# Moving the pieces of projections and feed-forward among the 64 slots of a batch

## Chip, cores and metric

The kernel runs on one core of a Trainium2 chip. The metric is the device time of one execution in microseconds (us), the median of the runs shown. All of the work is one program; eight batches are computed one after the other.

## What is computed

For each of 8 batches with 1024 tokens of 256 features:

```python
xn = layernorm(x)
# attention branch, 16 heads of 16 features
u, v, q, k = split(silu(xn @ W1 + b1), 4)              # each 1024 x 256
scores = q_h @ k_h.T                                    # per head, 1024 x 1024
attn   = silu(scores) / S
y_attn = layernorm((attn @ v_h) * u, gamma, beta) @ W2 + b2
# feed-forward branch, hidden width 1024, ternary weights
h = gelu(layernorm(xn, g1, b1) @ ternary(w1).T + fb1)
y_ffn = layernorm(h, g2, b2) @ ternary(w2).T + fb2
out = x + y_attn + y_ffn
```

Everything is float32. Products that need the accuracy are split into a high and a low part in fp32r and summed over several matmul passes.

## The kernel before, in words

The attention of one batch is cut into `GROUPS` = 64 groups, called slots here. A slot g (function `scores`, L890 to L905) multiplies 128 keys with 512 queries for four pairs of heads: four matmuls, two at a time, into the four PSUM banks `scores`. ScalarE turns these into `attn` with two Silu activations of 128x1024 each (`silu_group`, L538). TensorE multiplies them with `V` one slot later (`times_v`, L907 to L923: four matmuls of 32 columns, written as eight instructions for two output positions in the profile's merged rows). There is one set of score banks: the first half of the next scores waits for the first Silu of this slot, the second half for the second.

Between `scores(g)` and `times_v(g-1)` TensorE issues the steps that row g of `TABLE` names. The same table is walked by ScalarE, VectorE and GpSimd, each doing its own part of a step in the table's order (`body` of each engine; SyncE has a fixed order of its own, L429 to L443). So the table is a schedule written out by hand, and every engine is strictly in order. The steps are:

- `xn.i`, `xt.i` (i = 0 to 3): normalise 256 tokens of the next batch, transpose them, split them into `xp` (L710, L948, L564, L820).
- `k.c.h`, `q.c.h`, `u.c.h`, `v.i`: projections (L958, L967); ScalarE applies Silu to k, q, u (L544), VectorE splits k and q into parts (L826, L828) and moves v to `vraw` (L836). `vs.c` places v in `V` on ScalarE (L556).
- `y.i`, `f1.t.h`, `gelu.i`, `ln2.i`, `nrm2.i`, `g.t.r`, `f2.t`: the feed-forward branch. `y` (L766 to L773, VectorE) is its input, `f1` the first product in two halves for each of 8 token tiles, evacuated at L779, `gelu` two tiles at once on ScalarE (L582, with a table load before and after it), `ln2` the statistics (L696, L700, and GpSimd L480, L482), `nrm2` the normalisation (L791), `g` four transposes (L985) with three VectorE operations (L796, L801, L803), `f2` the second product with 16 matmuls (L992), added to `part` (L807).
- `zt.i`, `zs.i`, `a.i`: the end of the previous batch's attention branch: transpose for the statistics (L1002, L732, L736), split (L741, L743), the product with W2 (L1008), added to `part` (L750).
- `px` (L757): `part` is set to x plus a constant for the present batch. It waits until the output of the previous batch has been stored (L756, `s_out`).

TensorE's pieces (`zt a u f1 g f2 xt k q v`) use two PSUM banks `fill` in turn. A piece waits for the evacuation of the piece two before it.

k and q do not go straight to the matmuls. SyncE writes the parts `kst` and `qst` to scratch in HBM (`write_parts`, L396 and L399, two DMAs each) and, after both have landed, reads them back in the layout of the score matmuls (`load_stack`, L416 and L419, ten DMAs) for one half c of the heads and one half h of the tokens. `scores` of slot 0 waits for stack (0,0), slot 4 for stack (0,1), slots 32 and 36 for (1,0) and (1,1). Stacks (0,0) and (0,1) of a batch are made from `k.0.0 q.0.0` and `k.0.1 q.0.1` in the last slots of the batch before. All these DMAs go through SyncE's one queue, in order: the stacks, `load_x`, and the two stores of the previous batch's output (L427), which wait for `a.1` and `a.3`.

Batches 1 to 6 are a hardware loop (`Fori`, L878 for VectorE and the same on the other engines), batch 0 and batch 7 are written out before and behind it. A prologue (`PRO`) runs the steps for the first batch (`ln1 xn xt k.0 q.0 v vs.0`) in the order in which they stand in the table, an epilogue (`EPI`) the steps `zs zt a` of the last.

The change and the steps of the prediction touch `TABLE` (L58 to L123), and through it the order of everything above. Which piece uses which `fill` bank follows from its place in the table (`bank_of`, L171).

Of the kernel before, what the change touches and what calls it, by code (L numbers as in the profile page):

```python
# [56 lines left out]

TABLE = (  # L58
    "zs.0 zt.0 zs.1 zt.1",
    "a.0 zs.2",  # L60
    "a.1",
    "zt.2",
    "zs.3 zt.3",
    "a.2",
    "vs.1 a.3 u.1.0 k.1.0 y.0",
    "q.1.0",
    "u.1.1",
    "k.1.1",
    "u.0.1 px q.1.1 u.0.0 y.2",
    "f1.0.0",  # L70
    "f1.0.1",
    "y.1",
    "",
    "f1.1.0 f1.1.1 y.3 gelu.0",
    "f1.2.0 f1.2.1",
    "ln2.0",
    "nrm2.0",
    "f1.3.0 g.0.0",
    "g.0.1",
    "f1.3.1 f2.0",  # L80
    "g.1.0",
    "g.1.1 gelu.1 f1.4.0 f1.4.1",
    "ln2.1 f2.1 f1.5.0",
    "nrm2.1 f1.5.1",
    "g.2.0",
    "g.2.1",
    "f2.2",
    "g.3.0",
    "",
    "",  # L90
    "g.3.1 f1.6.0 gelu.2",
    "f2.3 f1.6.1 f1.7.0",
    "ln2.2 f1.7.1",
    "",
    "",
    "nrm2.2 ln1",
    "",
    "g.4.0",
    "g.4.1 xn.0",
    "f2.4 g.5.0 g.5.1 gelu.3 xt.0",  # L100
    "f2.5 xn.1",
    "xt.1",
    "ln2.3",
    "nrm2.3",
    "k.0.0",
    "g.6.0 xn.2",
    "g.6.1",
    "q.0.0",
    "f2.6",
    "g.7.0",  # L110
    "g.7.1",
    "xt.2",
    "xn.3 v.0",
    "v.1 xt.3",
    "",
    "",
    "",
    "f2.7",
    "k.0.1",
    "q.0.1",  # L120
    "v.2",
    "v.3 vs.0",
)  # L123
SLOTS = [[(n.split(".")[0], *map(int, n.split(".")[1:])) for n in row.split()] for row in TABLE]
assert len(SLOTS) == GROUPS
# [981 lines left out]
```

## Time and profile before

| what | value |
|---|---|
| median of 3 runs | 1669.28 us (1665.27 to 1671.85) |
| the profiled execution | 1665.21 us, its span 1663.4 us |
| TensorE busy | 1542.5 us, 93% of the span |
| ScalarE busy | 1226.5 us, 74% |
| VectorE busy | 896.1 us, 54% |
| GpSimd busy | 98.6 us, 6% |
| mean granted TensorE clock | 0.982 of 2.4 GHz |
| Silu of the scores, L538 | 1024 activations, 985.3 us |
| `times_v` L921 and `scores` L902 | 550.9 and 414.9 us busy (overlapping pairs and fours) |

How to read it: an engine that is busy 93% of the span is not at its peak, because matmuls are pipelined and their ends are modelled. A slot is therefore measured here from the start of its first score matmul to that of the next slot's; the rows of the timeline give these starts. In the timeline, "idle before" in square brackets is the time for which the engine waited, and behind the arrow stands what ended it; "issue" is a wait for nothing that the profile shows. PE is TensorE, PEld its weight loads, DVE VectorE, ACT ScalarE, POOL GpSimd, SPq the DMA issues of SyncE.

### The profile page before, as it was taken

Reading aid. Unit: us, or ns where it says so; the run is one execution under the profiler, and the core shown is the slowest. Engines: PE = TensorE matmul, PEld = TensorE weight load, DVE = VectorE, ACT = ScalarE, POOL = GpSimd, SP = SyncE. Lnnn points to the kernel's source line nnn. Section 1 sums busy time; section 2 is a strip of 40 time slices with the busy share of each in tenths; the row PEclk is TensorE's granted clock in tenths of the full one; section 3 lists DMA queues with packets and bytes.
Section 4 is the critical chain, followed back from the end, with each engine's and each line's share of the span. In section 5 each row is a group of like instructions: output and inputs, shape, how many; then the busy total and the mean of one; then the engine's idle time right before and its main releaser. Section 6 shows DMA issues by size and latency. Waiting matters only on the chain.

```text
span 1663.4 us, 27784 instructions
## 1 busy us (share of the span) xinstructions
PE 1542.5 (93%) x9826; PEld 760.8 (46%) x9826; DVE 896.1 (54%) x1716; ACT 1226.5 (74%) x1285; POOL 98.6 (6%) x193
## 2 busy tenths in 40 slices
PE   4799999999899998999989999799997999999997
PEld 3345445444454444444444444444444454544443
DVE  5365735666257553576435664366634657346553
ACT  2378877788668886778857797587875788767884
POOL 2000100000000100001000010000100001000000
PEclk9799999999999999999999999999999999999999
DMA  6470044601544034430335203361034700346000
GB/s 192 90 151 27 6 88 115 123 26 38 110 99 87 26 68 87 127 77 1 77 90 134 57 1 77 90 152 39 1 79 101 152 26 13 88 103 127 1 1 26
DMA packets 62330, 123.68 MB, mean 74 GB/s; under 512 B 7664, under 2 KB 9328, under 8 KB 61168
## 3 DMA queue, kind: packets, MB, share of 16 engines
q1 hardware_dynamic: 62192, 121.81, 32.2%
q8 instruction: 90, 1.47, 0.4%
q14 instruction: 48, 0.39, 0.1%
HBM read 79.84 MB, written 41.94 MB: 73 GB/s over the span
## 4 chain that ended last, share of the span: by engine, by line
issue 75%; PE 15%; POOLq 4%; ACT 3%; DMA 1%; DVE 1%; POOL 1%; SPq 0%; DVEq 0%; ACTq 0%
PE outs L921 5%; PE scores L902 4%; ACT attn L538 2%; POOLq L505 2%; PE fill L992 2%; PE fill L976 1%; PE fill L958 1%; PE fill L985 1%; POOLq L497 1%; POOL rs L491 1%; POOLq L481 1%; DMA QS<-q_scratch 1%; PE fill L1008 0%; DMA q_scratch<-qst 0%; PE fill L967 0%
## 5 line engine op out<-in xcount | busy, mean ns | idle before, releaser
L538 ACT ACTIVATE attn<-scores 128x1024 f32<-128x1024 f32 x1024 | 985.3, 1025 | 361.3 <-PE scores L902 360.9
L921 PE MATMUL outs<-attn,V 128*32 128x512 f32 x4096 | 550.9, 610 | 0.3 <-ACT attn L538 0.3
L902 PE MATMUL scores<-QS,KS 64*128 64x512 f32 x2048 | 414.9, 467 | 57.4 <-ACT attn L538 28.6
L902 PEld LDWEIGHTS scores<-QS,KS 64*128 64x128 f32 x2048 | 172.6, 186 | 533.8 <-ACT attn L538 391.7
L796 DVE TENSOR_TENSOR tmp<-fill,l2g 128x512 f32<-128x512 f32 x128 | 88.5, 691 | 129.6 <-PE fill L985 125.9
L921 PEld LDWEIGHTS outs<-attn,V 128*32 128x32 f32 x4096 | 81.2, 109 | 129.8 <-issue 118.3
L992 PE MATMUL fill<-Wq,hgh 128*128 128x256 f32 x512 | 131.5, 295 | 0.6 <-DVE tmp L796 0.5
L958 PE MATMUL fill<-xp,W1h 128*128 128x512 f32 x384 | 127.9, 415 | 3.0 <-DVE xp L820 3.0
L779 DVE SCALAR_TENSOR_TENSOR hid<-fill,ratq,fb1b 128x512 f32<-128x512 f32 x128 | 96.1, 751 | 61.5 <-PE fill L976 50.8
L992 PE MATMUL fill<-Wq,hgl 128*128 128x256 f32 x512 | 125.2, 282 | 0.0
L992 PEld LDWEIGHTS fill<-Wq,hgh 128*128 128x128 f32 x512 | 97.2, 190 | 18.9 <-issue 16.7
L807 DVE SCALAR_TENSOR_TENSOR part<-fill,cq,part 128x256 f32<-128x256 f32 x64 | 31.0, 484 | 136.2 <-PE fill L992 135.1
L480 POOL TENSOR_TENSOR rp<-mv,epst 128x2 f32<-128x2 f32 x64 | 12.5, 195 | 1500.5 <-DVE mv L700 961.8
L992 PEld LDWEIGHTS fill<-Wq,hgl 128*128 128x128 f32 x512 | 97.4, 190 | 0.3
L803 DVE TENSOR_TENSOR hgl<-tmp,hgh 128x512 fp32r<-128x512 f32 x128 | 88.6, 692 | 9.9 <-issue 0.4
L985 PE MATMUL fill<-ident,hid 128*128 128x128 f32 x512 | 83.4, 285 | 2.9 <-DVE hid L791 1.8
L696 DVE BATCH_NORM_STATS2 st<-hid 128x6 f32<-128x512 f32 x128 | 79.1, 681 | 10.6 <-issue 5.6
L958 PEld LDWEIGHTS fill<-xp,W1h 128*128 128x128 f32 x384 | 67.4, 190 | 35.2 <-issue 22.5
L958 PE MATMUL fill<-xp,W1l 128*128 128x512 f32 x192 | 75.7, 394 | 0.0
L985 PEld LDWEIGHTS fill<-ident,hid 128*128 128x128 f32 x512 | 54.1, 141 | 40.1 <-issue 37.0
L976 PE MATMUL fill<-Wq,yX 128*128 128x512 f32 x256 | 72.2, 413 | 0.0
L976 PE MATMUL fill<-Wq,yT 128*128 128x512 f32 x256 | 71.2, 410 | 0.0
(110 smaller groups left out, 1383.2 us busy)
## 6 DMA issues: line engine op xcount, KB each, us to landing
QS<-q_scratch SPq DMA_DIRECT2D x128, 256.0 KB, 7.2
k_scratch<-kst SPq DMA_DIRECT2D x64, 256.0 KB
q_scratch<-qst SPq DMA_DIRECT2D x64, 256.0 KB
KS<-k_scratch SPq DMA_DIRECT2D x64, 256.0 KB, 4.9
KS<-k_scratch SPq DMA_DIRECT2D x128, 128.0 KB, 5.7
xin<-in_x SPq DMA_DIRECT2D x8, 1024.0 KB, 4.8
out_dram<-part SPq DMA_DIRECT2D x16, 512.0 KB, 2.7
w1raw<-in_W SPq DMA_DIRECT2D x1, 1024.0 KB, 7.1
```

What stands on the lines that cost most here:

```text
L505: pool.drain()
L538: nc.scalar.activation(attn[:, g % 2, 2 * hf:2 * hf + 2, :], SP[:, 2 * hf:2 * hf + 2, :], ACT.Silu).then_inc(s_silu, 1)
L696: V_.bn_stats(st[:, j, n, :] if len(views) > 1 else st[:, j, :], v)
L779: V_.scalar_tensor_tensor(out=hid_of(t)[:, cols], in0=FP[:, k, :], scalar=ratq[:, t:t + 1], in1=fb1b[:, cols], op0=ALU.mult, op1=ALU.add). ...
L796: V_.tensor_tensor(tmp[:, :].rearrange("p (c n) -> p c n", n=P), FP[:, k, :].rearrange("p (c n) -> p c n", n=P), l2g[:, 4 * r:4 * r + 4].u ...
L803: V_.tensor_tensor(hgl[:, r, :], tmp[:, :], hgh[:, r, :].bitcast(F32), ALU.subtract).then_inc(s_hg, 1)
L902: ins = mm(SP[:, j, :], KS[rows, pair, t * P:(t + 1) * P], QS[rows, pair, h * HALF:(h + 1) * HALF], start=True, stop=True)
L921: ins = mm(OP[32 * j:32 * j + 32, g // RUN % 2, :], V[:, t, c * HPC // 2 + j, o * DH:o * DH + 2 * DH], attn[:, g % 2, n, :], start=(o == 0 ...
L958: ins = mm(bank.rearrange("p (i n) -> p i n", i=2), w[:, kc, col:col + P], xp[:, 2 * h:2 * h + 2, part, kc, :], start=n == 0, stop=n == le ...
L976: ins = mm(bank, y_of(t // 2)[:, part, kc, t % 2 * P:(t % 2 + 1) * P], Wq1[:, kc, hf * HALF:(hf + 1) * HALF], start=n == 0, stop=n == len( ...
L985: ins = nc.tensor.transpose(bank[:, n * P:(n + 1) * P], hid_of(t)[:, col:col + P], ident[:, :])
L992: ins = mm(bank[:, 0:D], w[:, r, n * P:(n + 1) * P], Wq2[:, 4 * r + n, :], start=i == 0, stop=i == len(passes) - 1)
```

## The change

Only `TABLE` changes. The same 96 steps of a batch stand in other rows; none is added or dropped. Rows with no entry go from 9 to 10. The `f2` rows stand further apart in the middle of the batch. `k.0.1` and `q.0.1`, which had rows 60 and 61, both go into row 63, behind `v.3`; `vs.1` goes from row 6 to 2, `zt.3` from 4 to 3, `px` from row 10 to 6, `y.2` and `y.1` into one row 10; the feed-forward pieces `f1.0.1` to `f1.2.1` stand together in row 15 with `gelu.0`. `k.1.0`, `q.1.0` and `q.1.1` move from rows 6, 7 and 10 to 7, 8 and 13, `k.1.1` stays in row 9. Rows without a piece of TensorE (empty ones and those with only `ln1`, `nrm2` and the like) are 13 instead of 15. In the prologue's order, `v.0` now comes ahead of `xt.1` and `k.0.0`, and `v.2 v.3` ahead of `k.0.1 q.0.1`.

```diff
--- before.py
+++ after.py
@@ -57,69 +57,69 @@
 
 TABLE = (
     "zs.0 zt.0 zs.1 zt.1",
-    "a.0 zs.2",
-    "a.1",
-    "zt.2",
-    "zs.3 zt.3",
+    "a.0",
+    "vs.1 zt.2",
+    "zs.2 a.1 zt.3 zs.3",
     "a.2",
-    "vs.1 a.3 u.1.0 k.1.0 y.0",
+    "a.3",
+    "px u.0.0 y.0",
+    "k.1.0",
     "q.1.0",
-    "u.1.1",
     "k.1.1",
-    "u.0.1 px q.1.1 u.0.0 y.2",
+    "y.1 y.2 u.1.1",
+    "u.0.1",
+    "u.1.0",
+    "q.1.1",
     "f1.0.0",
-    "f1.0.1",
-    "y.1",
+    "f1.0.1 f1.1.0 f1.1.1 gelu.0 f1.2.0 f1.2.1",
+    "y.3 ln2.0 f1.3.0",
     "",
-    "f1.1.0 f1.1.1 y.3 gelu.0",
-    "f1.2.0 f1.2.1",
-    "ln2.0",
+    "",
     "nrm2.0",
-    "f1.3.0 g.0.0",
+    "g.0.0",
     "g.0.1",
-    "f1.3.1 f2.0",
-    "g.1.0",
-    "g.1.1 gelu.1 f1.4.0 f1.4.1",
-    "ln2.1 f2.1 f1.5.0",
-    "nrm2.1 f1.5.1",
+    "f1.3.1 f2.0 gelu.1 g.1.0 g.1.1",
+    "f1.4.0",
+    "ln2.1 f1.4.1",
+    "nrm2.1 f2.1",
     "g.2.0",
-    "g.2.1",
+    "g.2.1 f1.5.0",
     "f2.2",
     "g.3.0",
+    "g.3.1",
+    "f1.5.1",
+    "f1.6.0 f2.3 gelu.2 ln2.2 f1.6.1",
+    "nrm2.2 f1.7.0",
     "",
     "",
-    "g.3.1 f1.6.0 gelu.2",
-    "f2.3 f1.6.1 f1.7.0",
-    "ln2.2 f1.7.1",
+    "ln1",
     "",
     "",
-    "nrm2.2 ln1",
-    "",
-    "g.4.0",
-    "g.4.1 xn.0",
-    "f2.4 g.5.0 g.5.1 gelu.3 xt.0",
-    "f2.5 xn.1",
-    "xt.1",
-    "ln2.3",
+    "xn.0 g.4.0",
+    "f1.7.1 gelu.3 g.4.1",
+    "f2.4 g.5.0 g.5.1",
+    "xt.0 xn.1",
+    "f2.5 ln2.3",
+    "v.0",
     "nrm2.3",
-    "k.0.0",
-    "g.6.0 xn.2",
+    "g.6.0",
     "g.6.1",
-    "q.0.0",
+    "xt.1 xn.2",
     "f2.6",
     "g.7.0",
+    "k.0.0",
+    "q.0.0",
     "g.7.1",
-    "xt.2",
-    "xn.3 v.0",
-    "v.1 xt.3",
     "",
     "",
     "",
+    "xt.2",
+    "v.1",
+    "",
     "f2.7",
-    "k.0.1",
-    "q.0.1",
+    "xn.3 xt.3",
     "v.2",
-    "v.3 vs.0",
+    "v.3 k.0.1 q.0.1 vs.0",
 )
 SLOTS = [[(n.split(".")[0], *map(int, n.split(".")[1:])) for n in row.split()] for row in TABLE]
 assert len(SLOTS) == GROUPS
```

## Rows read from the trace of the kernel before

**Rows 1.** Windows, scores 4 to 63: length, busy PE, PEld, DVE, ACT, POOL; clock; DMA.
```profile
1072.64:1250.51 177.87, 173.86 (x1121) 84.81 (x1117) 100.32 (x188) 142.03 (x149) 9.69 (x19) 1.00 0.28 66
...
1471.30:1641.22 169.92, 164.80 (x1041) 75.74 (x1042) 83.25 (x145) 136.57 (x140) 4.45 (x10) 0.98 0.20 41
```

**Rows 2.** The same view, scores 63 to scores 4 of batch 1; sum of all seven.
```profile
248.80:265.59 16.79, 14.85 (x113) 8.10 (x110) 10.71 (x26) 10.74 (x12) 2.67 (x6) 1.00 0.85 181
...
sum 155.05, PE 112.76 PEld 61.58 DVE 68.03 ACT 74.83 POOL 14.24; mean PE 16.11 PEld 8.80 DVE 9.72 ACT 10.69 POOL 2.03
```

**Rows 3.** Timeline (start, duration, engine, line, operation): scores 48 to 51, batch 3.
```profile
801.07 0.79 PE L902 MATMUL scores<-QS,KS 64*128 64x512 f32 x4
...
803.37 0.73 PE L902 MATMUL scores<-QS,KS 64*128 64x512 f32 x4
...
806.62 0.73 PE L902 MATMUL scores<-QS,KS 64*128 64x512 f32 x4
...
810.38 0.73 PE L902 MATMUL scores<-QS,KS 64*128 64x512 f32 x4
```

**Rows 4.** The same view, scores of slots 56 and 59 of batch 5.
```profile
1230.70 0.73 PE L902 MATMUL scores<-QS,KS 64*128 64x512 f32 x4
...
1236.48 0.49 PE L902 MATMUL scores<-QS,KS 64*128 64x512 f32 x2
```

**Rows 5.** The same view, scores of slots 11 and 12 of batch 3.
```profile
693.51 0.73 PE L902 MATMUL scores<-QS,KS 64*128 64x512 f32 x4
...
696.30 0.73 PE L902 MATMUL scores<-QS,KS 64*128 64x512 f32 x4
```

**Rows 6.** Timeline, batch 5, slot 10 with three projections, scores 10 and 11.
```profile
1094.03 0.73 PE L902 MATMUL scores<-QS,KS 64*128 64x512 f32 x4
...
1099.10 0.69 ACT L544 ACTIVATE uz<-fill,b1s 128x512 f32<-128x512 f32 x1 [0.61 <-PE fill L958]
...
1099.99 0.73 PE L902 MATMUL scores<-QS,KS 64*128 64x512 f32 x4
```

**Rows 7.** Timeline, ScalarE around a Gelu, slots 14 to 16 of batch 5.
```profile
1113.32 1.92 ACT L582 ACTIVATE hid<-hid 128x2048 f32<-128x2048 f32 x1
...
1116.56 3.77 ACT L538 ACTIVATE attn<-scores 128x1024 f32<-128x1024 f32 x4
```

**Rows 8.** Timeline, VectorE and DMA issues, from batch 5 to batch 6.
```profile
1248.28 1.20 SPq L399 DMA_DIRECT2D q_scratch<-qst  x2
...
1253.61 1.25 SPq L416 DMA_DIRECT2D KS<-k_scratch  x3
...
1258.10 0.43 DVE L741 CAST yT<-uz 128x512 fp32r<-128x512 f32 x1 [4.51 <-issue]
...
1266.44 0.25 DVE L736 BATCH_NORM_AGGREGATE mv<-st 128x2 f32<-128x6 f32 x2 [6.22 <-issue]
```

**Rows 9.** Timeline, loads and scores 4 and 5 of batch 7.
```profile
1456.44 1.26 SPq L416 DMA_DIRECT2D KS<-k_scratch  x3
...
1471.30 1.22 PE L902 MATMUL scores<-QS,KS 64*128 64x512 f32 x4 [3.16 <-DMA QS<-q_scratch]
...
1475.36 1.22 PE L902 MATMUL scores<-QS,KS 64*128 64x512 f32 x4
```

**Rows 10.** Timeline, DMA issues of the prologue and the first scores.
```profile
24.42 1.37 SPq L396 DMA_DIRECT2D k_scratch<-kst  x2
...
26.47 1.43 SPq L399 DMA_DIRECT2D q_scratch<-qst  x2
...
32.75 1.29 SPq L416 DMA_DIRECT2D KS<-k_scratch  x3
...
46.50 1.22 PE L902 MATMUL scores<-QS,KS 64*128 64x512 f32 x4 [8.53 <-DMA QS<-q_scratch]
```

**Rows 11.** The group of px (count, busy us, mean ns, idle before), batches together.
```profile
L757 DVE TENSOR_TENSOR part<-xin,cst 128x2048 f32<-128x2048 f32 x8 | 18.3, 2292 | 1.6 <-issue 1.3
```

**Rows 12.** Line L427, the stores of the output, all sixteen.
```profile
DMA to landing us min/median/max: 2.6/2.7/6.0
```

## Prediction: the change, step by step

> **What bounds the kernel now.** I cut the span at two score matmuls of each batch, those of slot 4 and of slot 63, and read both stretches in the view of busy time by windows. From scores 4 to scores 63 a batch takes 177.87 us with TensorE busy for 173.86 of them [rows 1]. This is a stretch bound by TensorE, with some time given to ScalarE. From scores 63 to scores 4 of the next batch the seven crossings take 155.05 us together, but the one into batch 1, which has no jump back in the loop, only 16.79 [rows 2]. So the six others have a mean of 23.0: there the kernel waits. The timeline of a crossing with a jump shows VectorE idle for 4.51 and 6.22 us for "issue", that is for nothing it was to be given [rows 8]. The timeline of batch 7 shows scores 4 held 3.16 us by the load of the stack [rows 9]. Two waits compete there: the instruction stream of VectorE behind the jump, and the chain `q.0.1`, write, load.
>
> Inside the long stretch I read slot lengths from the starts of the scores. A slot with one `g` takes 2.30 us, with one projection 3.25, with one `f2` 3.76 [rows 3], with one `f1` 2.79 [rows 5]. Three slots without a piece take 5.78 [rows 4], 1.93 each, and three projections in one slot 5.96 [rows 6]. Two constants fit these: the scores and `times_v` cost TensorE 1.66 us, a slot that has any piece 0.15 more, and the pieces 0.45 (`g`, `xt`, `zt`), 0.98 (`f1`), 1.45 (`k q u`, also `v` and `a`) and 1.96 (`f2`). A run of slots without a piece costs more than 1.66 each, since ScalarE then sets the pace.
>
> The Trainium skill, "Runtime: NRT & Kernel Launch", section "Instruction fetch mechanics", says that a taken branch breaks the sequential prefetch and forces a fetch, and that crossing a block otherwise is mostly hidden. The first of VectorE's two waits agrees with it. The second, 6.22 us behind a few instructions of the loop, does not look hidden, and the trace decides. By that rule only the first wait would be left, and the crossings of the changed kernel would be set by the load all the more; the sum below does not use it.
>
> **The change, part by part.**
>
> *Slots 4 to 62.* Before, 59 slots x 1.66 = 97.9, 44 slots with a piece x 0.15 = 6.6, pieces 65.6, together 170.1. The measured 177.9 leaves 7.8 us of excess, where ScalarE or an evacuation is late. After, `k.0.1`, `q.0.1` (2 x 1.45) and `zt.3` (0.45) have left, so the pieces are 62.2, the slots with a piece 46 (6.9), together 167.0. The excess I put together anew. Runs without a piece: slots 17 to 19 1.0, slots 34 to 38 1.55, slots 54 to 56 with the next slot 1.25, the single ones 45 and 59 0.1; the three-slot run of before gives the scale, 5.78 - 3 x 1.66 = 0.8 and a remainder in the next slot [rows 4]. Gelu: it takes 3.24 us from its start to the next Silu [rows 7] with the table load behind it. `gelu.0` in slot 15 has 5 `f1` beside it and slot 16 one more, so it costs nothing (if that cover went, about 1 us); `gelu.1` 0.3; `gelu.3` in slot 40 with only `f1.7.1 g.4.1` 0.75. In slots 22, 41 and 15 the third piece wants the bank whose evacuation is just under way: 0.25 each, 0.8 together. Bounds for this excess are 4.5 and 10 us; the nearest row is before's own 7.8. So far 5.75.
>
> `px` is moved to slot 6, right behind `a.3`. It waits for the store of the output, which SyncE issues only when `a.3` is evacuated and which lands 2.6 us later at best [rows 12], whereas before `px` hardly waited, 1.6 us in eight times [rows 11]. Queued behind it on VectorE are `y.0` and the split of `k.1.0`. With `px` (2.29 us [rows 11]) and `y.0` (five operations on half as many or fewer elements, taken as 2.8 us with their drains) the split ends some 9.5 us into slot 6, the write of `kst` some 5 us after that, and `k.1.1` in slot 9, which overwrites `kst`, has ScalarE wait some 2.5 us. Most of it is slack of a slot of 3.25; 0.75 remains. Bounds 0 and 2.
>
> Excess after: 6.5, stretch 173.5, that is -4.4 per batch. For batches 0 to 6: -30.8. The last batch has no `k.0.1` and `q.0.1` in either kernel, and takes 169.92 us [rows 1]; there only `zt.3` and the smaller excess count: -1.7.
>
> *Scores 63 to scores 4.* Slot 63 now holds `v.3 k.0.1 q.0.1`. The third of three projections reaches ScalarE 5.07 us after the slot's scores [rows 6], and its Silu (0.69) and the split on VectorE end at 7.0 (a cast of the size that takes 0.43 [rows 8] and a subtraction, taken as 1.2). Then come the writes. Before, where `k.0.1` and `q.0.1` stand in neighbouring slots of 3.25 us [rows 3], the loads start 5.33 us after the latter [rows 8]. In the prologue, with 2.05 us between them, they start 6.28 after it, 8.33 after the first [rows 10]. Now the two are 1.35 us apart, nearer to the prologue: taking 8.33 from the first, the loads start at 14.0 us from the scores. From the first load to the scores that wait for it the prologue shows 13.75 us [rows 10] and batch 7 14.86 [rows 9]; I take 13.9. So scores 4 come at 27.9 to 28.0 us after scores 63, in every crossing, with a jump or without. Seven times 27.95 are 195.65, against 155.05 now: +40.6. Bounds: 5.33 from the second write (issued at 7.0) and 13.75 for the loads give 26.1 (-13 in all), 14.86 gives 28.9 (+6.7).
>
> Is the other wait later? VectorE jumps when the split of `q.0.1` is done, at 7.0, resumes 4.5 later and passes the second wait 8.34 after that [rows 8], at 19.8. `zs.1`, `zt.1`, then `zt.2`, `a.1` and `zt.3` on TensorE follow, some 8 us. That ends at 27.9 as well: the load hides VectorE's waits almost exactly, and what now costs 23.0 in the mean costs 28.
>
> *Clock.* In batch 7, scores 4 to 5 take 4.06 us [rows 9] where a slot with one transpose takes 2.30 [rows 3]: after the wait the clock granted is at its lower level, and slots 4 and 5 lose about 2.5 us. The crossing into batch 1 has a clock of 1.00 throughout [rows 2]; with 9 us of wait it will not. The other crossings already have a low stretch. I add 2 for batch 1 and 0.5 for each of five: 4.5. Bounds 0 and 12.
>
> *Start.* In the prologue `v.0` goes ahead of `xt.1` and `k.0.0`. TensorE is there at the lower clock and half waiting: +2.1 us to the first scores (0 to 3), nothing for the second stack, which queues behind the first.
>
> Sum: -30.8 - 1.7 + 40.6 + 4.5 + 2.1 = +14.7 us. On the profiled execution (1665.21 us) that is 1680; it lies 4 us under the median of 1669.28, and on the median it is 1684, +0.9%.
>
> **The rivals.**
> 1. *The forecast*: crossings of 28 us, 60%. Its own range is 1675 to 1698.
> 2. *The load comes sooner, the clock doesn't fall further*: crossings at 26 us (7 x -1.95 = -13.7) and no clock term: 1684 - 18 = 1666. With half of this 1675. For it: nothing else is in the queue when `kst` and `qst` are written. Against it: the prologue's 8.33 was also measured in a queue with nothing ahead. 22%.
> 3. *VectorE's instructions are last*: its second fetch meets the stack's loads, which now start later, and each of five jump crossings grows by 2 to 4 us: 1684 + 15 = 1699. It decides when VectorE's second wait ends later than 20 us after scores 63. 8%. The Trainium skill, "DMA: Bandwidth & Descriptors", has each DMA engine go round its queues packet by packet, so that a fetch would wait for little; here the second wait is 6.22 us beside the loads [rows 8], and the trace decides.
> 4. *Faster*: the one mechanism is the excess in slots 4 to 62. If the fuller slots hide ScalarE and VectorE so well that only the runs (3.9 us) remain, each of eight batches gains 2.6 more, -21, and with crossings of 27 us 1684 - 21 - 7 = 1656. It decides when the stretch is under 171.5 us. For it: before's `gelu.1` and `gelu.2` cost nothing. Against it: before's slots with a third piece do wait. 10%.
>
> **How the numbers follow.** The likeliest case gives 1684. A measurement of this kernel tells about 0.5% (8.3 us) from no change. Below 1661 is case 4, most of it: faster 0.09. Between 1661 and 1677.6 are case 2 and the lower edge of the forecast: 0.26. Above: 0.65. The range 1665 to 1700 leaves out most of case 4 and the upper edge of 3.
>
> **What would show it.** In the profile after: scores 4 held by the load of QS in all seven crossings, each 27 to 29 us from scores 63, with or without a jump; the stretch from scores 4 to scores 63 at 173.5; VectorE idle before `px` for about 2.9 us, ended by the store; slots 17 to 19 at 5.9 us. The forecast falls if crossings stay under 25.5 us or the stretch is off by more than 2.5 us.

## The result, and the profile after

The changed kernel takes 1707.23 us in the median of four executions (1701.35 to 1707.83), beside 1667.28 us for the kernel before on the same chip: a ratio of 1.0231 [1.0194, 1.0268], so 2.3% slower, and clear of no change. The forecast was 1684 (+0.9%), range 1665 to 1700: the sign was right, the size was not. The profiled execution took 1707.83 us with a span of 1706.0, against 1665.21 and 1663.4 before; the parts below are of these two spans, whose difference is 42.6 us. The mean clock granted to TensorE fell from 0.982 to 0.972.

The same cuts as in [rows 1, 2], in the view of busy time by windows: first scores 63 to scores 4 of the next batch (the crossing into batch 1, one with a jump, the last, the sum of all seven), then scores 4 to scores 63 of batches 5, 6 and 7. Columns: length; busy PE, PEld, DVE, ACT, POOL; clock; DMA share; GB/s.

```profile
246.69:277.73 31.04, 18.14 (x128) 10.55 (x125) 14.00 (x34) 12.92 (x16) 3.56 (x8) 0.87 0.58 118
...
1278.88:1307.43 28.55, 19.54 (x128) 11.81 (x125) 14.00 (x34) 13.03 (x16) 3.56 (x8) 0.94 0.58 128
1484.20:1511.86 27.66, 18.16 (x128) 10.55 (x124) 13.89 (x34) 12.93 (x16) 3.56 (x8) 0.88 0.58 132
sum 203.47, PE 136.00 PEld 80.01 DVE 97.89 ACT 91.00 POOL 24.93; mean PE 19.43 PEld 11.43 DVE 13.98 ACT 13.00 POOL 3.56
...
1103.57:1278.88 175.31, 171.63 (x1101) 82.05 (x1102) 95.60 (x176) 139.03 (x144) 8.39 (x15) 1.00 0.30 64
1307.43:1484.20 176.77, 173.06 (x1100) 83.20 (x1100) 95.58 (x176) 139.04 (x144) 8.42 (x15) 0.99 0.28 64
1511.86:1683.41 171.55, 165.91 (x1037) 75.89 (x1037) 82.29 (x141) 135.67 (x138) 3.56 (x8) 0.98 0.19 41
sum 1413.38, PE 1382.67 PEld 658.45 DVE 752.21 ACT 1109.37 POOL 62.10; mean PE 172.83 PEld 82.31 DVE 94.03 ACT 138.67 POOL 7.76
```

The crossings grew from 155.05 us [rows 2] to 203.47, that is +48.4, more than the whole loss. They are about equally long with a jump in the loop (28.6 to 29.6) and without one (31.0 and 27.7). The long stretches gave back only 8.1 (1413.4 against 1421.5), the start to the first scores cost 2.3, slots 0 to 3 of batch 0 gave 0.5, and the end cost 0.4.

One crossing in the timeline (start, duration, engine, line, operation, idle time before it), from scores 63 of batch 5 to slot 6 of batch 6:

```profile
1278.88 0.73 PE L902 MATMUL scores<-QS,KS 64*128 64x512 f32 x4
...
1284.66 1.21 SPq L396 DMA_DIRECT2D k_scratch<-kst  x2
...
1286.01 1.92 SPq L399 DMA_DIRECT2D q_scratch<-qst  x2
...
1291.77 0.43 DVE L741 CAST yT<-uz 128x512 fp32r<-128x512 f32 x1 [5.79 <-issue]
...
1293.81 1.25 SPq L416 DMA_DIRECT2D KS<-k_scratch  x3
...
1295.03 0.25 DVE L736 BATCH_NORM_AGGREGATE mv<-st 128x2 f32<-128x6 f32 x2 [1.13 <-issue]
...
1300.26 0.75 PE L902 MATMUL scores<-QS,KS 64*128 64x512 f32 x4
...
1307.43 1.22 PE L902 MATMUL scores<-QS,KS 64*128 64x512 f32 x4 [3.36 <-DMA QS<-q_scratch]
...
1312.18 0.74 PE L902 MATMUL scores<-QS,KS 64*128 64x512 f32 x4
...
1315.46 0.73 PE L902 MATMUL scores<-QS,KS 64*128 64x512 f32 x4
```

Counted from scores 63, the write of `qst` is issued at 7.13 us, the loads start at 14.93, and scores 4 start at 28.55, held by the load of QS. VectorE has passed its second wait at 16.15, and that wait is 1.13 us instead of the 6.22 of [rows 8]. Slot 4, which has one `a` piece, takes 4.75 us (1307.43 to 1312.18), its scores at the lower clock level (1.22 us instead of 0.73); slot 5, with one `a` at the full clock, takes 3.28.

From the view of waits of the changed kernel (engine, line, waited for: us in total, times, longest). Before, `px` hardly waited [rows 11] and `kst` did not wait for a DMA:

```profile
PE scores L902 <- DMA QS<-q_scratch: 50.3, 9, 12.3
DVE yT L741 <- issue: 29.7, 7, 6.0
...
ACT kst L544 <- DMA k_scratch<-kst: 23.1, 8, 3.6
DVE part L757 <- DMA out_dram<-part: 20.8, 7, 3.7
DVE mv L736 <- issue: 5.6, 5, 1.1
```

And the timeline behind `px` in batch 6, with the scores of slots 10, 11, 12 and 13 at 1328.46, 1332.44, 1336.38 and 1339.63:

```profile
1318.39 2.29 DVE L757 TENSOR_TENSOR part<-xin,cst 128x2048 f32<-128x2048 f32 x1 [2.85 <-DMA out_dram<-part]
...
1325.06 1.24 SPq L396 DMA_DIRECT2D k_scratch<-kst  x2
...
1328.46 0.73 PE L902 MATMUL scores<-QS,KS 64*128 64x512 f32 x4
...
1330.79 0.69 ACT L544 ACTIVATE kst<-fill,b1s 128x512 f32<-128x512 f32 x1 [3.09 <-DMA k_scratch<-kst]
...
1332.44 0.50 PE L902 MATMUL scores<-QS,KS 64*128 64x512 f32 x2 [0.66 <-ACT attn L538]
...
1336.38 0.73 PE L902 MATMUL scores<-QS,KS 64*128 64x512 f32 x4
...
1339.63 0.73 PE L902 MATMUL scores<-QS,KS 64*128 64x512 f32 x4
```

`px` waits 2.85 us for the store, the write of `kst` goes out at 1325.06, and the Silu of `k.1.1` cannot overwrite `kst` before 1330.79. ScalarE stands 3.09 us, its Silus of the scores of slots 9 and 10 are late, and slots 10 and 11 take 3.98 and 3.94 us instead of 3.25.

### The profile page after: what moved, and what is told of

It is laid out like the page before. It is cut to its first block, busy times and chain, and to the rows that moved or that the text cites. A ratio compares the mean times of both kernels' runs of the same rounds, so it can differ in the third digit from the quotient of the medians.

```text
span 1706.0 us, 27801 instructions
## 1 busy us (share of the span) xinstructions
PE 1561.7 (92%) x9826; PEld 767.4 (45%) x9826; DVE 895.7 (53%) x1716; ACT 1222.5 (72%) x1285; POOL 101.5 (6%) x193
## 4 chain that ended last, share of the span: by engine, by line
issue 90%; POOLq 5%; PE 2%; POOL 1%; ACT 1%; DVE 1%; DVEq 0%; ACTq 0%
POOLq L505 3%; POOLq L497 1%; POOLq L481 1%; POOL rs L491 1%; ACT attn L538 1%; PE outs L921 1%; PE scores L902 1%; PE fill L992 0%; POOLq L499 0%; POOLq L490 0%; PE fill L985 0%; DVEq L725 0%; POOLq L495 0%; DVE st L732 0%; PE fill L1008 0%
## 5 line engine op out<-in xcount | busy, mean ns | idle before, releaser
L992 PEld LDWEIGHTS fill<-Wq,hgh 128*128 128x128 f32 x512 | 97.3, 190 | 16.2 <-issue 15.4
L696 DVE BATCH_NORM_STATS2 st<-hid 128x6 f32<-128x512 f32 x128 | 79.1, 681 | 15.1 <-ACT hid L582 11.6
L958 PEld LDWEIGHTS fill<-xp,W1h 128*128 128x128 f32 x384 | 66.4, 191 | 38.2 <-issue 28.6
L820 DVE TENSOR_TENSOR xp<-fill,xp 128x512 fp32r<-128x512 f32 x32 | 22.1, 692 | 92.5 <-ACT xp L564 92.5
```

Of the source, the lines that this page charges most:

```text
L696: V_.bn_stats(st[:, j, n, :] if len(views) > 1 else st[:, j, :], v)
L958: ins = mm(bank.rearrange("p (i n) -> p i n", i=2), w[:, kc, col:col + P], xp[:, 2 * h:2 * h + 2, part, kc, :], start=n == 0, stop=n == le ...
L992: ins = mm(bank[:, 0:D], w[:, r, n * P:(n + 1) * P], Wq2[:, 4 * r + n, :], start=i == 0, stop=i == len(passes) - 1)
```

## The experiments

**Theory.** The loss is the chain of slot 63: splits of `k.0.1` and `q.0.1`, their writes, the loads that wait for them, scores 4. The move of `px` adds a smaller loss of its own. **Rivals.** VectorE's wait behind the jump is what is last (then a kernel with no jump would be much faster); or the fuller slots and longer empty runs of the stretch cost the time (then putting `k.0.1` and `q.0.1` back would leave most of the loss).

### a_kq_back: the changed kernel, `k.0.1` and `q.0.1` back in slots of their own

```
@@ TABLE of after, rows 57 to 63
-    "xt.2",  "v.1",  "",  "f2.7",  "xn.3 xt.3",  "v.2",  "v.3 k.0.1 q.0.1 vs.0",
+    "xt.2",  "xn.3 v.1",  "xt.3 f2.7",  "k.0.1",  "q.0.1",  "v.2",  "v.3 vs.0",
```

> The changed kernel with k.0.1 and q.0.1 taken out of row 63 and put into rows 60 and 61, where they stood before; for that xn.3, xt.3 and f2.7 go up one to three rows (rows 57 to 63: xt.2 / xn.3 v.1 / xt.3 f2.7 / k.0.1 / q.0.1 / v.2 / v.3 vs.0). Theory 1 (the chain q.0.1, write, load sets the seven crossings from scores 63 to scores 4): the crossings go back from 203.5 to about 155 us, slot 4 loses its slow clock (-11), the stretch from scores 4 to 63 gets the two projections back (+2.9 in each of seven, +20): about 1668, 1.000 of before. Theory 2 (the changed kernel is slower because of its fuller slots and runs without a piece): the crossings stay over 190 and the time stays over 1695.

Measured: 1674.84 us, ratio 1.0038 [1.002, 1.0055]. So 1.9 of the 2.3% come from these few rows. Its seven crossings and their sum:

```profile
sum 165.79, PE 123.87 PEld 66.26 DVE 71.33 ACT 82.70 POOL 19.41; mean PE 17.70 PEld 9.47 DVE 10.19 ACT 11.81 POOL 2.77
```

The crossings without a jump are back at 16.91 and 16.48 us, and the five with one are 24.4 to 27.1: both of VectorE's waits are back (4.07 and 6.08 us in the crossing into batch 6). They are still 10.7 us longer in all than before. The changed first rows are the likely reason, which no run separates: there slot 3 has `zs.2 a.1 zt.3`, so more of slot 3 stands behind VectorE's second wait, from whose end to scores 4 this kernel takes 11.6 us (1272.79 to 1284.35) and the one before 8.9.

### b_kq_late: the kernel before, `k.0.1` and `q.0.1` moved into row 63

```
@@ TABLE of before, rows 59 to 63
     "f2.7",
-    "k.0.1",  "q.0.1",  "v.2",  "v.3 vs.0",
+    "",  "",  "v.2",  "v.3 k.0.1 q.0.1 vs.0",
```

> The kernel before with one thing of the change: k.0.1 and q.0.1 moved from rows 60 and 61 (left empty) into row 63 behind v.3. Theory 1: crossings rise from 155 to about 203, rows 60 and 61 shrink from 6.5 to 4 us (-18 in seven), slot 4 is slowed by the clock (+11): about 1667 + 48 - 18 + 11 = 1708. Theory 2, that VectorE's waits for instructions behind the jump set the five loop crossings anyway: only the two crossings without a jump grow, by 12 us each: about 1673.

Measured: 1703.23 us, 1.0221 [1.0191, 1.0251]. One move in the old table gives about as much loss as the whole change.

```profile
sum 199.34, PE 132.37 PEld 76.86 DVE 90.59 ACT 84.55 POOL 18.70; mean PE 18.91 PEld 10.98 DVE 12.94 ACT 12.08 POOL 2.67
```

Its crossings are 28.0 to 29.1 us, all seven. With the run before this settles the place of the loss. The rival of the fuller slots is out: this kernel has the old ones.

### a_px_back: the changed kernel, `px` back in row 10

```
-    "px u.0.0 y.0",
+    "u.0.0 y.0",
...
-    "y.1 y.2 u.1.1",
+    "px y.1 y.2 u.1.1",
```

> The changed kernel with px alone moved back from row 6 to row 10 (px y.1 y.2 u.1.1). Theory 1: px no longer waits for the stored output, the split of k.1.0 and its write come some 5 us sooner, ScalarE no longer waits at k.1.1, slots 10 and 11 go from 3.97 and 3.93 to 3.25 each: -10 to -12 us, about 1696, 1.016 of before. Theory 2 (slots 10 and 11 are long because VectorE has y.1 and y.2 there): no change, since px is then added to the same slot, or slower.

Measured: 1692.84 us, 1.0153 [1.013, 1.0177], about 0.8% better than the changed kernel. `px` no longer waits for the store. The stretches sum to 1398.8 us instead of 1413.4, slots 10 and 11 take 3.25 each, and the crossings stay long, at 199.5. About 12 of the 14.6 us are slots 10 and 11; most of the rest is slot 4, which lost 2.3 us less to the lower clock in this execution. ScalarE's wait is nearly gone, from 23.1 us to 6.6:

```profile
ACT kst L544 <- DMA k_scratch<-kst: 6.6, 8, 0.9
```

### b_unrolled and a_unrolled: no jump

Each of the five engines' loops over batches 1 to 6 is written out; nothing else differs.

```
-            with dve.Fori(1, NB - 1) as b:
+            for b in range(1, NB - 1):
```

> The kernel before with the hardware loop over batches 1 to 6 written out on all five engines; nothing else. If the waits for issue behind the jump are the fetch of instructions at a jump, the five crossings of 22 to 26 us fall to the 16.8 to 18 us of the two without a jump: -33 us, about 1634, 0.980 of before. If they are something that every crossing from a batch of the middle has (the store, the loads of the stack), nothing changes: 1667.

Measured: 1624.29 us, 0.9733 [0.9708, 0.9759]. The stretches are unchanged (1421.42), the crossings fall from 155.05 to 120.73:

```profile
sum 120.73, PE 103.87 PEld 56.68 DVE 74.22 ACT 75.14 POOL 18.92; mean PE 14.84 PEld 8.10 DVE 10.60 ACT 10.73 POOL 2.70
```

So what bounded the crossings of the kernel before was VectorE's wait behind the jump, and some 6 to 7 us sooner stands the load: five crossings with a jump had a mean of 24.0 us, and written out the same five have 17.5.

> The changed kernel with the hardware loop written out. Written out, the kernel before went to 0.973, its loop crossings from 24 to 17 us. Theory 1 (in the changed kernel the chain q.0.1, write, load is last and VectorE's waits for instructions lie beside it): the crossings stay at 28 to 29 us, only slot 63 loses its 1.3 us before the scores, which moves nothing; about 1703, at most 5 less. Theory 2 (the changed kernel's crossings are set by the jump as well): they fall by 5 to 7 us in five batches, about 1675.

Measured: 1699.34 us, 1.0208 [1.0169, 1.0247]. With the same edit the changed kernel gains almost nothing. Crossing into batch 6, from 1275.98:

```profile
1303.85 0.79 PE L902 MATMUL scores<-QS,KS 64*128 64x512 f32 x2 [9.65 <-DMA QS<-q_scratch]
```

The crossing is 27.87 us, nearly as with the loop, but now TensorE stands before the load for 9.65 us instead of 3.36. The jump is not what is last in the changed kernel; its rival is out.

### a_k_row62: only `k.0.1` one slot earlier

```
-    "v.2",
-    "v.3 k.0.1 q.0.1 vs.0",
+    "v.2 k.0.1",
+    "v.3 q.0.1 vs.0",
```

> The changed kernel with k.0.1 alone one row up (rows 62 and 63: v.2 k.0.1 / v.3 q.0.1 vs.0). The split of q.0.1 ends 1.4 us sooner after scores 63, and its write goes out some 4 us behind that of k.0.1 instead of 1.3. If the two writes queue behind one another (loads 7.2 to 8.2 us behind the q write, where 5.4 before), the loads start at about 11.1 us instead of 14.9, and the crossings shrink by 3.8 us, unless VectorE's chain behind the jump (resume, zs, zt, a) holds them at some 26: 3 to 4 us in seven crossings, less 1.4 that slot 62 gets: -10 to -17, 1690 to 1697. If the writes do not matter, only the 1.4 us move from slot 63 to 62: 1707.

Measured: 1692.30 us, 1.0165 [1.0133, 1.0197]. The crossing into batch 6, from scores 63 at 1268.41:

```profile
1269.46 1.21 SPq L396 DMA_DIRECT2D k_scratch<-kst  x2
...
1274.14 1.20 SPq L399 DMA_DIRECT2D q_scratch<-qst  x2
...
1279.99 1.25 SPq L416 DMA_DIRECT2D KS<-k_scratch  x3
...
1293.56 0.73 PE L902 MATMUL scores<-QS,KS 64*128 64x512 f32 x4 [1.79 <-DMA QS<-q_scratch]
```

With 4.7 us between the two pairs of writes, the loads start 5.85 us after the second (5.4 to 5.9 in all seven); with 1.35 us between them they start 7.80 after it (7.2 to 8.2). The second write is issued 1.4 us sooner and the loads follow it 2 us faster, and the crossings fall by 24 us to 179.37. The stretches give 7 of that back, mainly since slot 62 now has two projections (4.72 us instead of 3.32).

### b_small_load: a quarter of the bytes behind the jump

In the kernel before, the loads of stack (0, 1) move fewer pairs from batch 1 on; the ten DMAs and all waits stay. The kernel leaves out the new data of three pairs of heads in four, so it does not compute the result.

```
+                few = reused and (c, h) == (0, 1)
+                w = slice(0, 1 if few else PPC)
-                pairs = slice(c * PPC, (c + 1) * PPC)
+                pairs = slice(c * PPC, c * PPC + (1 if few else PPC))
...
-                                     kv[e, first:first + rows, :, cols])
+                                     kv[e, first:first + rows, w, cols])
```

> The kernel before, but from batch 1 on the ten DMAs of stack (0,1) load one pair of heads of four instead of all (a quarter of the bytes; the scores of the other three pairs then use older data, so the output is not the reference's). If VectorE's second wait behind the jump (6.2 us for issue) comes from its instruction fetch standing behind the loads, it shrinks to 1 or 2 us, as in the changed kernel, where the fetch is over before the loads begin; the loop crossings fall from 24 to some 18 to 19, those without a jump by the 2 us that scores 4 waited: -30, about 1637. If the second wait belongs to the jump alone, it stays at 4 to 6 us: crossings of 23, about 1660.

Measured: 1622.33 us, 0.9745 [0.9716, 0.9774], with the jump still there; the crossings sum to 114.6 and those with a jump take 17.0. That is 15 us under the expectation: the crossings gave 40 us instead of 30, since both of VectorE's waits got shorter than expected. VectorE's waits in two kernels, the one before:

```profile
DVE mv L736 <- issue: 27.2, 5, 6.2
DVE yT L741 <- issue: 22.5, 8, 4.7
```

and this one (whose line numbers are higher by 2):

```profile
DVE yT L743 <- issue: 18.6, 8, 3.6
...
DVE mv L738 <- issue: 1.5, 5, 0.4
```

The first wait is 3.5 us, the second is gone. Nothing of VectorE's work or of its jump was changed, only bytes in flight. The second wait needs both: without the jump it is gone, and without the bytes as well. So it is a fetch of instructions that stands behind the load's traffic. The page's table of queues, of the kernel before, has a queue of instructions (packets, MB, share):

```profile
q14 instruction: 48, 0.39, 0.1%
```

In the trace, packets of this queue start 5.2 and 13.2 us after scores 63 in the crossing into batch 6, and VectorE's two waits end at 7.6 and 15.9. In all five crossings with a jump each of the two waits ends 2.1 to 2.8 us after such a packet starts; the trace does not name the engine that a packet is for, so that they are VectorE's rests on these times. Behind the first wait the next packet starts 5.6 us later here, and 0.5 us later with a quarter of the bytes (7.1 after 6.6), while the packet itself takes under 1 us in both. Written out, the kernel has 42 of these packets instead of 48.

### a_both_unrolled, w_early_unrolled, w_early: what is best

The first puts back `px` and `k.0.1 q.0.1` in the changed table and writes the loops out.

> The changed kernel with k.0.1 and q.0.1 back in rows 60 and 61, px back in row 10, and the loop written out: what is left of the change is its arrangement of slots 4 to 62. Its stretch there should be 176 us (177.4 with k and q back, less 1.4 for px) against 178.5 of the kernel before written out, the crossings 17 in both: 0.965 of before, about 1610. If the arrangement itself gains nothing: 0.973, 1624.

Measured: 1617.25 us, 0.9719 [0.9694, 0.9743]. The crossings are 117.9. The stretches of batches 1 to 6 are 176.2 us (one 177.8, with a slow slot 4) where b_unrolled has 177.5 to 179.4: the new arrangement of the other pieces is 1.3 us shorter per batch, comparing those at the full clock. The times do not show it: 0.9719 and 0.9733 have intervals that overlap, and the 0.965 that was expected is not reached.

The second also has the load start before scores 63:

```
@@ TABLE of after, px in row 10, rows 54 to 63
+    "xt.2",  "xn.3 v.1",  "xt.3",  "f2.7",  "k.0.1",  "q.0.1",  "",  "v.2",  "",  "v.3 vs.0",
```

> The changed kernel, loop written out, px in row 10, and rows 54 to 63 rearranged: xt.2 / xn.3 v.1 / xt.3 / f2.7 / k.0.1 / q.0.1 / (none) / v.2 / (none) / v.3 vs.0. k.0.1 and q.0.1 stand two rows earlier than in the kernel before, and the run of three slots without a piece is gone. If the load of stack (0,1) is what is left of the wait in the crossings (16.9 us, 14.8 with a quarter of the load), they fall to about 15: -14; without the run and the long slot behind it each batch gains 1.2: -10. Together 1593 against 1617 with q.0.1 in row 61, 0.957 of before. If the crossing of 16.9 us is TensorE's own work, only the 10 us: 1607.

Measured: 1607.22 us, 0.9642 [0.9607, 0.9678], the fastest kernel of this study, 3.6% under the one before. Its crossings are 15.9 to 16.3 us with no wait for the load. Against a_both_unrolled the crossings gave 5.9 us where 14 were hoped for, and the stretches 3.6 where it was 10. The time is that of the second case of its expectation, 1607, but by other parts. The empty rows 60 and 62 bring little, since each slot with a `v` piece behind an empty one takes 3.9 us instead of 3.28, as slots 62 and 63 of batch 5 show (1.65 and 3.93):

```profile
1207.26 0.73 PE L902 MATMUL scores<-QS,KS 64*128 64x512 f32 x4
...
1208.91 0.50 PE L902 MATMUL scores<-QS,KS 64*128 64x512 f32 x2
...
1212.84 0.49 PE L902 MATMUL scores<-QS,KS 64*128 64x512 f32 x2
```

The third is the same table with the loops kept.

> The same table with the hardware loop kept. The jump is there, and the loads of stack (0,1), which start some 5.4 us behind the split of q.0.1 in row 59 and take 14, are still under way for its first 8 us or so. If VectorE's fetch waits for the loads in flight, its second wait is shorter than the 6.2 us of the kernel before but not gone: loop crossings of about 20 us, 1618, 0.970. If any load in flight costs the whole wait: crossings of 24, 1638.

Measured: 1651.72 us, 0.9911 [0.9884, 0.9937]. The loads start 0.5 to 0.9 us before scores 63 and land 12.6 to 14.7 us after them, and yet a crossing with a jump takes 24.1 to 25.2 us. The one into batch 6, from 1244.90:

```profile
1254.82 1.22 PE L902 MATMUL scores<-QS,KS 64*128 64x512 f32 x4 [5.92 <-issue]
...
1257.99 0.43 DVE L741 CAST yT<-uz 128x512 fp32r<-128x512 f32 x1 [9.37 <-issue]
...
1260.67 0.25 DVE L736 BATCH_NORM_AGGREGATE mv<-st 128x2 f32<-128x6 f32 x2 [0.56 <-issue]
```

The load now hits the first fetch instead of the second, and TensorE's own as well. The two waits of VectorE together are 9.9 us here and 10.7 in the kernel before: in these two kernels the loads' bytes cost about the same, whichever fetch they meet. The kernel is 0.9% faster than the one before through its stretches (1406.2 in all, crossings 155.6); the expectation of shorter crossings failed.

## Why the prediction was right and wrong

**In short.** The mechanism was right and the sum was too small. Four of its terms were mis-sized, all to the same side: the excess in slots 4 to 62 (about 10 us), the time from the writes to the loads in the crossings (7.8), the wait behind `px` (6) and the clock behind the wait (4.1).

**What bounds the kernel.** Right. The two competing waits were the right ones, and b_unrolled and b_small_load show the instruction stream as last before, b_kq_late the load as last after.

**Crossings, forecast +40.6, measured +48.4.** The mechanism held: all seven held by the load of QS, with a jump or without. The split of `q.0.1` ends at 7.11 us (7.0 forecast). The mis-sized term is the one between write and load. I took 8.33 us from the first write, since the prologue shows that [rows 10]; measured are 8.6 to 9.6 from the first and 7.2 to 8.2 from the second, so the loads start at 14.4 to 15.4 instead of 14.0. Of these three gaps the shorter had the longer second time: 5.33 with 3.25 us between [rows 8], 6.28 with 2.05 [rows 10], 7.2 to 8.2 with 1.35. Had I taken this series on to 1.35 instead of holding its sum fixed, I would have had about 7. In a_unrolled it is 7.3 to 7.5 in all seven crossings, so up to 0.7 us of the 8.2 may come with the loop. From the first load to scores 4 it then took 13.3 to 15.7 us, where I took 13.9, with the larger values in the first crossings. The crossings into batches 1, 2 and 4 (31.04, 29.57 and 29.26) lie above the 27 to 29 that I named.

**VectorE, forecast to end at the same 27.9.** Wrong, without a price. I carried over the 8.34 us from its first to its second wait. After the change the packet of VectorE's second fetch starts 3.2 us after that of the first instead of 8.0, since it comes before the loads' traffic is there; TensorE was ready 25.2 us after scores 63 (3.36 before scores 4). Rival 3 needed the end of that wait past 20 us; it came at 16.15.

**Clock, forecast +4.5, measured about +8.6.** Slot 4 lost 2.5, 2.6, 1.5, 1.4, 0, 1.5 and 1.6 us in batches 1 to 7, 11.1 together, against the 2.5 that batch 7 lost before. I gave the five crossings with a jump 0.5 each, on the ground that they already had a low stretch. The granted clock of these windows was 0.86 to 0.93 before and 0.88 to 0.94 after, so that was true; but before, the stretch was over when scores 4 came (the full clock from slot 4 on, 2.25 to 2.30 us), and now the low level lies behind the wait, on scores 4 and slot 4. It was within the bounds of 0 to 12.

**Slots 4 to 62, forecast -32.5 apart from the clock.** Measured, with the 8.6 of the clock taken out, is -16.7. Of batches 1 to 6 only batch 5 stayed within 2.5 us of the 173.5; the others are at the point where the forecast was to fall. Two terms failed. The wait behind `px`: 0.75 us per batch forecast with bounds of 0 and 2, measured 1.3 to 1.7 in batches 1 to 6, none in batch 0, which has no store before it, and 3.5 in batch 7, 12.1 in all instead of 6. The order of the events was as told: `px` waited 2.85 us (2.9 forecast), and `kst` 3.09 (2.5). What failed is "most of it is slack of a slot": only about half of the wait was. a_px_back gives that time back. The rest, about 1.2 us per batch, is the excess: 6.9 in batch 5, which has no slow slot 4, where I had 5.75. Slots 17 to 19 took 5.79 us (5.9 forecast), but the first slot with a piece behind empty ones was longer than its pieces:

```profile
1361.10 0.49 PE L902 MATMUL scores<-QS,KS 64*128 64x512 f32 x2
...
1361.80 0.50 PE L902 MATMUL scores<-QS,KS 64*128 64x512 f32 x2 [0.21 <-ACT attn L538]
...
1363.81 0.73 PE L902 MATMUL scores<-QS,KS 64*128 64x512 f32 x4
...
1474.26 0.50 PE L902 MATMUL scores<-QS,KS 64*128 64x512 f32 x2
...
1475.13 0.49 PE L902 MATMUL scores<-QS,KS 64*128 64x512 f32 x2 [0.37 <-ACT attn L538]
...
1478.64 0.73 PE L902 MATMUL scores<-QS,KS 64*128 64x512 f32 x4
```

Slot 20, with one `g`, takes 2.71 us instead of 2.25 to 2.30, and slot 60, with one `f2` behind a single empty slot, 4.38 instead of 3.76; slots 46 and 57 have 0.64 and 0.45 over. I had charged empty runs mostly by their own length, with a remainder for one of them. The rows show what most of it is: the second half of the scores starts 0.70 us (slot 20) and 0.87 us (slot 60) after the first, held by ScalarE's Silu, where it is 0.34 in a slot behind one with a piece. Slots 57 and 46 have the same 0.70 and 0.87. TensorE ran ahead in the empty slots, and the first slot with a piece pays for ScalarE's lag.

**Start.** +2.3 against +2.1, right.

**Together.** The crossings missed by 7.8, the clock by 4.1, `px` by 6, the excess by about 10: 28 us, which is the 42.6 measured less the 14.7 forecast. All four had the same sign. All four stood in the text with bounds that held the measured value in the mean, or nearly did (for the crossings, a sum of 47.3 against 48.4); the range added too little of them at once. They are not independent: a longer wait also lowers the clock behind it.

**The rivals.** 2 (the load sooner) is out, the load came later. 3 is out, as told. 4 is out: the stretch was 175.3 to 178.1 in batches 1 to 6, not under 171.5.

**The two rules.** That a taken branch breaks the prefetch (the Trainium skill, "Runtime: NRT & Kernel Launch", section "Instruction fetch mechanics") agrees: without the jumps both waits of VectorE are gone. The second wait, which the prediction left to the trace, is a fetch too, and b_small_load shows what it stands behind. What rival 3 drew from the other rule, that a fetch would wait for little, does not come out here: the second wait is 4.3 to 6.2 us beside the whole load and at most 0.4 beside a quarter of its bytes.

## What to carry to other kernels

When a producer, its write to memory and the load back stand between two stages, count the chain from the last producer to the first consumer at the place it is moved to, and count two writes that follow as closely as here (1.35 us) as a queue, not as a pair. Where a loop jumps, look at what is in the DMA queues at that moment: here the jump and 2 MB of loads beside it cost 2.7% together, and writing the loop out takes that away; moving fewer bytes at that moment would too, if the kernel can spare them. An empty slot is not free time where ScalarE is behind: the next piece pays part of it back.

## What the runs showed of the hardware that was not expected

- The wait for instructions behind a jump grows with the DMA traffic in flight. In the crossing into batch 6 VectorE waited 3.5 us and 0.4 at most a second time beside a quarter of the bytes, 4.5 and 6.2 beside the whole load (4.3 to 6.2 the second time in all five), 5.8 and 1.1 beside the writes, with the load coming after them, and 9.4 and 0.6 when the load was already under way. TensorE, which did not wait so long in the other kernels (1.8 us before), waited 5.9 then.
- The time from a 512 KB pair of writes to the loads that wait for it depends on the pair ahead: 5.4 to 5.9 us with 4.7 us between, 7.2 to 8.2 with 1.35. In the changed kernel the ten loads of a stack, 2 MB, took 13.2 to 15.6 us from the first issue to the last landing.
- A wait of TensorE can cost twice: the 3.4 us before scores 4 of batch 6 were followed by a slot that was 1.5 us longer at the lower of the two clock levels (its scores took 1.22 us instead of 0.73). Not every wait does: behind the 2.3 us before scores 4 of batch 5 slot 4 ran at the full clock, 3.28 us.
